# Attention over a graph's edges and the sums over edges behind it: another layout of the sums, one product on another engine, and another order of loads

## The chip, the cores and the metric

The kernel runs on one core of one Trainium2 chip. The metric is the device time of one execution in microseconds (us). Engines are named as the profile names them: PE is TensorE's matmul, PEld its weight load, DVE is VectorE, ACT is ScalarE, POOL is GpSimd and SP is SyncE, which here only issues transfers.

## The reference, cut to what matters

The program is a stack of eight layers over N = 3125 nodes with C = 256 features and E = 53125 edges. Three of them bear on the change. Layer 0 is attention over edges; layer 1's graph part and the two convolutions of layer 3's add, for every node, the rows of its neighbours times a weight of the edge:

```python
# layer 0: attention over edges (4 heads of 64)
e = attn_src[:, src_idx] + attn_dst[:, dst_idx]
e = jnp.where(e >= 0, e, NEG_SLOPE * e)
e = e * edge_weight[None, :]
e_exp = jnp.exp(e - jnp.max(e))
denom = jax.ops.segment_sum(e_exp.T, dst_idx, num_segments=num_nodes).T
alpha = e_exp / (denom[:, dst_idx] + 1e-10)
msg = h[:, src_idx] * alpha[..., None]
out = jax.vmap(lambda m: jax.ops.segment_sum(m, dst_idx, num_segments=num_nodes))(msg)
...
# layer 1, and twice in layer 3: a weighted sum over the edges
msg = x[src] * edge_weight[:, None]
agg = jax.ops.segment_sum(msg, dst, num_segments=x.shape[0])
```

## The kernel before

**Attention** (`attend_edges`). The edges lie sorted by their end in 25 rounds of 2125. In a round POOL gathers 17 tiles of rows by index (L1120), ACT makes masks from the ends of the edges, `dst_all` (L1181, L1183), PE adds the ends' terms (L1346), DVE makes the logits (L1262 to L1269), a maximum goes through PE and back (L1353, L1274), DVE scales the rows (L1283) and PE adds them up by node (L1371) with masks `spread` of DVE (L1255). Three sets of buffers go round. At the end DVE makes each node's share, `den` (L1324 to L1327), multiplies all the sums by it (L1329) and adds them to X (L1330).

SP's queue holds, beside the transfer of `dst_all` for each round (L1151), the loads of *blocks*. A block is the edges of five nodes, up to 125 of them; there are 625 blocks, and 630 loads of 120 rows (L1158) put them on chip, 30 for each of the rounds 0 to 20. What SP does is what its queue says, in order. When the loads are there, `block_keys` (L790) turns ends and starts into the numbers that the next stage compares. `begin_rest` and `pick_rest` (L750, L764) look for blocks with more than 120 edges.

**Counts and sums over edges** (`count_edges`). 125 batches of KB = 5 blocks. In a batch DVE makes one-hot rows of the starts, `low` (L885), and of the ends with the rest of the start, `cell` (L886), and the product of `low` with the edges' weights, `heavy` (L872, in `weighs`). PE multiplies `cell` by `low` into counts (L935) and `heavy` by `cell` into sums (L941); ACT copies both out of PSUM (L968, L973) to `total` and `sums`, the latter of 128 x 3125 numbers for a group of five batches. SP stores them in `edge_counts` and `edge_sums` (L995), a group at a time. The buffers between DVE and PE have five slots. Then a loop runs over the blocks with a rest: DVE marks the block as done and looks for the next (L911 to L773), the block's old counts and sums are loaded (L1014, L1015), added to (L919, L920) and stored again (L1017, L1018).

A block's sums have 125 columns: number d*25 + t stands for end d of the block (of 5) and part t of the starts (of 25).

**Aggregates** (`aggregate`, three times). It reads `edge_sums` back and multiplies: for each group and each half of the features 25 matmuls, one for each t, of a tile of features with the sums of that t (L728). Their moving operand has 250 columns (two groups x 25 blocks x 5 ends) of 4 bytes each:

```python
last = pe.matmul(acc[:, m, h, 0:groups * GD], M[:, t, h * 128:(h + 1) * 128], heavy[m][0:P, 0:groups, t],
                 start=(t == 0), stop=(t == T - 1))
```

Every such part of the program is a phase, and each phase ends with a barrier of all engines (L90). So the count loop starts when attention's last instruction is done.

Of the kernel before, what the change touches and what calls it, by code (L numbers as in the profile page):

```python
# [18 lines left out]
F32 = mybir.dt.float32  # L19
# [29 lines left out]
LOADED = 21  # L49
HELD = LOADS * LOADED  # L50
# [615 lines left out]
class SumsLoads(Ahead):  # L666


    def __init__(self, nc, stack, name, weights):
        super().__init__(nc, stack, name)  # L670
        self.first = self.sb("first", [128, 2, T, GD])
        self.weights = weights
# [6 lines left out]
def aggregate(nc, g, weights, M, AT, loads, turn=1, last=True, ahead=()):  # L679

    with Phase(nc) as ph:
        heavy = (loads.first, ph.sb("second", [ROWS, 2, T, GD]))
# [33 lines left out]
        def _(pe):  # L716
# [73 lines left out]
def block_keys(dve, then, own, based):  # L790


    src, dst = (own.edges[:, 0:BLOCKS, k] for k in (1, 0))
    then(dve.tensor_copy(own.spare, src))
# [5 lines left out]
    then(dve.tensor_copy(own.spare, dst))  # L800
# [7 lines left out]
def count_edges(nc, g, edges, own, counts, weights):  # L808
# [6 lines left out]
    with Phase(nc) as ph:  # L815
        low = ph.sb("low", [EB, SLOTS, KB, ROWS])
# [3 lines left out]
        sums = ph.sb("sums", [ROWS, 2, T, GD])  # L820
# [6 lines left out]
        old_counts = ph.sb("old_counts", [P, P], U16)  # L827
        added = ph.sb("added", [1, BLOCKS])
# [10 lines left out]
        sums_stored = [ph.sem(f"sums_stored{m}") for m in range(2)]  # L839
        rest_read = ph.sem("rest_read")  # L840
# [10 lines left out]
        old_sums = sums[0:P, 1]  # L851
# [17 lines left out]
        def weighs(eng, n, k):  # L869
            at = k % SLOTS  # L870
            eng.wait_ge(low_ready, n + 1)
            eng.tensor_tensor(heavy[:, at], low[:, at], own.edges[:, bass.ds(n * KB, KB), 2:3].bitcast(F32).to_broadcast([EB, KB, ROWS]),  # L872
                              ALU.mult).then_inc(heavy_ready, 1)


        @block.vector
        def _(dve):
            dve.sem_inc(batch_summed, SLOTS)
            dve.sem_inc(counts_kept, TURNS)
            dve.sem_inc(batch_kept, TURNS)  # L880
# [8 lines left out]
            over_batches(dve, one)  # L889

            rests = rest_total(dve)
            with dve.Fori(0, rests) as v:
                then = Steps(dve, rest_step, v * REST)
                b = dve.value_load(g.pick_i[0:1, 0:1], min_val=0, max_val=BLOCKS - 1)
                place = nc.s_assert_within(b % BG, 0, BG - 1, skip_runtime_bounds_check_because="a block's place in its group")
# [24 lines left out]
                then(dve.tensor_tensor(old_sums[:, :, bass.ds(place * BLK, BLK)], old_sums[:, :, bass.ds(place * BLK, BLK)],  # L920
                                       acc[0:P, 0, 1, 0, 0:P].rearrange("p (d h) -> p h d", h=T), ALU.add))
# [4 lines left out]
        def _(pe):  # L926
            def one(n, k, i):
# [29 lines left out]
        def _(act):  # L957
            def one(n, k, i):
# [21 lines left out]
        def _(sp):  # L980
# [22 lines left out]
            store(GROUPS - 1, 0)  # L1003
            for m in range(2):
                sp.wait_ge(sums_stored[m], 16 * (GROUPS // 2) + 32 - 16 * m)
                sp.wait_ge(stored[m], 32 * (GROUPS // 2) + 64 - 32 * m)
            with sp.Fori(0, rests) as v:
# [9 lines left out]
                sp.dma_start(old, old_sums.rearrange("p h d -> p (h d)")).then_inc(rest_stored, 16)  # L1017
# [12 lines left out]
SETS = 3  # L1030
# [3 lines left out]
def attend_edges(nc, g, table, a_dst, dst_flat, dst_row, edges, own_blocks, X):  # L1034
# [5 lines left out]
    with Phase(nc) as ph:  # L1040
# [20 lines left out]
        total = ph.sb("total", [P, T, W])  # L1061
        den = ph.sb("den", [P, T, HEADS])
# [80 lines left out]
        def _(sp):  # L1143
# [77 lines left out]
        def _(dve):  # L1221
# [1811 lines left out]
```

## Time and profile before

| | |
|---|---|
| median of 3 runs | 5204.59 us (5191.33, 5204.59, 5204.67) |
| profiled execution | 5195.46 us, span 5193.8 us |
| PE busy | 4168.2 us, 80% of the span |
| DVE busy | 2408.1 us, 46% |
| ACT busy | 1855.3 us, 36% |
| POOL busy | 862.5 us, 17% |
| mean granted TensorE clock | 0.883 of full speed |

The shares are means over many stages, each with a limit of its own. Attention runs from about 107 to 834.9 us of the span, the count loop to 1116.1 and its loop over rests to 1155.9 us, the first aggregate from 1524.4 to 1790.9 us, the two others from 4239 us on. Within a stage what counts is the engine that the others wait for.

### The profile page before, as it was taken

The page shows a single profiled execution, that of the slowest core. Times are in us where ns is not written, and L with a number is a line of the kernel's source. Part 1 is how long each engine was busy: PE and PEld are TensorE (multiplying, and loading weights), DVE is VectorE, ACT ScalarE, POOL GpSimd, SP SyncE. Part 2 cuts the span into 40 slices and gives each one's busy share as a digit, 9 for nine tenths or more (in the row PEclk, how much of TensorE's full clock was granted, in tenths as well). Part 3 has the DMA queues.
Part 4 walks back from the last instruction along what each step waited for, and adds up shares of the span by engine and source line. Part 5 has one row for each costly group of instructions (what it writes and reads, how often), then busy time and mean ns, then how long its engine had stood idle before and what let it go on. Part 6 is the DMA issues. An engine that isn't in the chain of part 4 may idle for free. (4 is left out here: it accounts for less than half of the span.)

```text
span 5193.8 us, 79246 instructions
## 1 busy us (share of the span) xinstructions
PE 4168.2 (80%) x22693; PEld 3605.1 (69%) x22694; DVE 2408.1 (46%) x4239; ACT 1855.3 (36%) x3178; POOL 862.5 (17%) x796
## 2 busy tenths in 40 slices
PE   2588877955749976967997998997499969899675
PEld 2476767954638843866886886886499858788554
DVE  5355558965340032126995995897411140110424
ACT  2333323642410032424664664665143310110322
POOL 2577770002600010210000000000122200000101
PEclk8688888986969988988998998998599979999788
DMA  3344432542343211321221221221312144133000
GB/s 102 84 114 116 121 90 98 214 172 64 107 140 148 86 33 38 125 72 41 57 54 33 58 57 32 54 56 24 91 60 80 51 132 159 75 150 148 13 18 27
DMA packets 459231, 440.36 MB, mean 85 GB/s; under 512 B 347128, under 2 KB 411341, under 8 KB 446050
## 3 DMA queue, kind: packets, MB, share of 16 engines
q1 hardware_dynamic: 423868, 341.36, 21.6%
q0 software_dynamic: 35232, 97.61, 6.5%
q8 instruction: 38, 0.62, 0.0%
q14 instruction: 93, 0.76, 0.0%
HBM read 342.44 MB, written 96.42 MB: 84 GB/s over the span
## 5 line engine op out<-in xcount | busy, mean ns | idle before, releaser
L2575 PE MATMUL p_acc<-p_H,p_eT 125*125 125x256 f32 x3750 | 823.6, 379 | 0.0
L2575 PEld LDWEIGHTS p_acc<-p_H,p_eT 125*125 125x125 f32 x3750 | 696.2, 187 | 105.0
L1120 POOL DMA_INDIRECT p_message<-edge_table,p_index x425 | 495.1, 1165 | 170.5 <-issue 119.5
L1371 PE MATMUL p_acc<-p_message,p_spread 125*125 125x260 f32 x1666 | 427.9, 424 | 33.9 <-issue 29.1
L2059 DVE BATCH_NORM_STATS2 features_stats<-F x60 | 29.2, 487 | 868.0 <-ACT F L2050 867.3
L1371 PEld LDWEIGHTS p_acc<-p_message,p_spread 125*125 125x125 f32 x1666 | 349.9, 212 | 104.1 <-issue 36.2
L1830 ACT ACTIVATE p_hid<-p_up,p_b1s 128x125 f32<-128x125 f32 x764 | 272.2, 365 | 398.4 <-PE p_up L1806 355.0
L1806 PEld LDWEIGHTS p_up<-p_xT,p_w1s 128*128 128x128 f32 x3056 | 377.6, 199 | 50.1 <-issue 33.8
L1806 PE MATMUL p_up<-p_xT,p_w1s 128*128 128x125 f32 x3056 | 385.0, 284 | 32.0 <-issue 14.0
L1814 PE MATMUL p_down<-p_w2s,p_hid 128*125 128x256 f32 x1528 | 361.3, 386 | 11.7 <-ACT p_hid L1830 10.5
L526 PE MATMUL p_turned<-identity,p_slot 125*128 125x125 f32 x400 | 89.1, 376 | 303.3 <-DVE p_slot L494 299.7
L1423 POOL IOTA p_order_i<- 125x200 int32 x3 | 1.1, 381 | 1974.9 <-SPq L88 1974.9
L2498 ACT ACTIVATE p_eT<-p_turned 125x500 f32<-125x500 f32 (+1 forms) x525 | 251.1, 539 | 203.2 <-PE p_turned L2568 186.5
L1814 PEld LDWEIGHTS p_down<-p_w2s,p_hid 128*125 128x125 f32 x1528 | 278.0, 190 | 58.1 <-ACT p_hid L1830 17.6
L740 ACT ACTIVATE AT<-p_acc 128x250 f32 (+1 forms) x78 | 28.9, 371 | 772.6 <-PE p_acc L728 772.6
L526 PEld LDWEIGHTS p_turned<-identity,p_slot 125*128 125x128 f32 x400 | 59.8, 188 | 333.1 <-DVE p_slot L494 330.0
L728 PE MATMUL p_acc<-sums_first,H 125*128 125x250 f32 (+1 forms) x1400 | 278.0, 359 | 5.4 <-PEq L721 5.4
L728 PEld LDWEIGHTS p_acc<-sums_first,H 125*128 125x128 f32 x1400 | 248.0, 189 | 34.0 <-PEq L718 6.2
L2428 DVE CUSTOM_DVE_ANT_0 p_e_room<-p_S,p_pen 125x3125 f32<-125x3125 f32 x75 | 256.2, 3416 | 19.2 <-DVE p_pen L2422 15.6
L2438 DVE SCALAR_TENSOR_TENSOR p_e_room<-p_e_room,p_H,p_e_low 125x3125 f32<-125x3125 f32 x75 | 260.0, 3467 | 10.2 <-ACT p_e_low L2484 9.0
L2447 DVE CUSTOM_DVE_ANT_0 p_e_room<-p_e_room,p_count 125x3125 f32<-125x3125 f32 x75 | 256.2, 3416 | 12.4 <-ACT p_e_room L2490 8.9
L2490 ACT ACTIVATE p_e_room<-p_e_room,p_minus 125x3125 f32<-125x3125 f32 x75 | 217.7, 2903 | 116.3 <-DVE p_e_room L2438 116.3
(492 smaller groups left out, 6794.8 us busy)
## 6 DMA issues: line engine op xcount, KB each, us to landing
sums_first<-edge_sums SPq DMA_DIRECT2D x39, 1562.5 KB
p_count<-edge_counts SPq DMA_DIRECT2D x375, 152.6 KB
p_second<-edge_sums SPq DMA_DIRECT2D x36, 1562.5 KB, 8.0
edge_sums<-p_sums SPq DMA_DIRECT2D x25, 1562.5 KB
edge_counts<-p_total SPq DMA_DIRECT2D x25, 683.6 KB
p_w1s<-in_L_ffn_W SPq DMA_DIRECT2D x16, 1024.0 KB
p_got<-made SPq DMA_DIRECT2D x25, 560.0 KB
p_dst_all<-dst_row SPq DMA_DIRECT2D x25, 531.2 KB
```

Of the source, the lines that this page charges most:

```text
L728: last = pe.matmul(acc[:, m, h, 0:groups * GD], M[:, t, h * 128:(h + 1) * 128], heavy[m][0:P, 0:groups, t], start=(t == 0), stop=(t == T - 1))
L1120: pool.indirect_dma_start(message[:, m, k, :], None, table, bass.IndirectOffsetOnAxis(ap=index[:, m, k:k + 1], axis=0)).then_inc(landed[m] ...
L1371: last = pe.matmul(at, spread[:, k], message[0:P, m, k], start=(k == 0), stop=(k == R_CH - 1))
L1806: last = pe.matmul(up[:, c % 4, 0:UN], w1s[:, s, h, c * 128:(c + 1) * 128], xT[:, h], start=(h == 0), stop=(h == KH - 1))
L1814: last = pe.matmul(down[:, 0:C], hid[:, c], w2s[:, s, c], start=(c == 0), stop=(c == HC - 1))
L1830: act.activation(hid[:, c], up[:, c % 4, 0:UN], ACT.Gelu, bias=b1s[:, s, c:c + 1]).then_inc(hid_ready, 1)
L2428: dve.tensor_tensor_reduce(out=e[:, s], in0=S[:], in1=pen[:], scale=1.0, scalar=0.0, op0=ALU.add, op1=ALU.max, accum_out=peak[:, s:s + 1]) ...
L2438: dve.scalar_tensor_tensor(out=e[:, k % 2], in0=e[:, k % 2], scalar=d_of(t), in1=e_low[:], op0=ALU.add, op1=ALU.max).then_inc(leaky_ready, 1)
L2447: dve.tensor_tensor_reduce(out=e[:, s], in0=e[:, s], in1=count[:, k % 3], scale=1.0, scalar=0.0, op0=ALU.mult, op1=ALU.add, accum_out=den[ ...
L2490: act.activation(e[:, s], e[:, s], ACT.Exp, bias=minus[:, s:s + 1]).then_inc(raised, 1)
L2498: act.activation(eT[:, r % 4, 0:n], turned[:, r % 4, 0:n * P].rearrange("p (a n) -> p a n", a=n), ACT.Copy).then_inc(run_kept, 1)
L2575: last = pe.matmul(acc[:, s, 0:C], eT[:, r % 4, a % 4], H[:, a, 0:C], start=(a == 0), stop=(a == T - 1))
```

## The change

What it does, in six parts:

1. `sums`, and with it `edge_sums`, keeps each block's 125 columns as they come out of PSUM, in place of putting together the columns of one t over all blocks. ACT's copy (L973) becomes contiguous. The aggregates' moving operand then takes every 25th number, 100 bytes apart.
2. `weighs` goes from DVE to POOL. `low` has 125 columns in place of 128, and the three last columns of `heavy` are cleared once.
3. The product of the sums with the share and the sum with X leave the end of attention. DVE does them a tile at a time in the count loop, two instructions of 125x256 after every fifth batch.
4. In SP's queue the load of `dst_all` for round r stands ahead of the loads of blocks of round r - 3, for every round; before, the loads of blocks of rounds 0, 1 and 2 stood ahead of `dst_all` of round 3. There are 660 loads of blocks in place of 630.
5. On DVE `begin_rest` stands behind round 18, `pick_rest` behind 19, the first half of `block_keys` (`block_lows`) behind 21 and the second behind 22, in place of all of the first two behind 22 and of `block_keys` behind 23.
6. The last group is stored batch by batch, and the loop over rests loads and stores 125x125 of the sums in place of 125x3125.

```diff
 def aggregate(nc, g, weights, M, AT, loads, turn=1, last=True, ahead=()):
...
-                        last = pe.matmul(acc[:, m, h, 0:groups * GD], M[:, t, h * 128:(h + 1) * 128], heavy[m][0:P, 0:groups, t],
+                        last = pe.matmul(acc[:, m, h, 0:groups * GD], M[:, t, h * 128:(h + 1) * 128], heavy[m][0:P, 0:groups, :, t],
...
 def count_edges(...):
-            eng.tensor_tensor(heavy[:, at], low[:, at], own.edges[:, bass.ds(n * KB, KB), 2:3].bitcast(F32).to_broadcast([EB, KB, ROWS]),
+            eng.tensor_tensor(heavy[:, at, :, 0:P], low[:, at], own.edges[:, bass.ds(n * KB, KB), 2:3].bitcast(F32).to_broadcast([EB, KB, P]),
                               ALU.mult).then_inc(heavy_ready, 1)
+
+        @block.gpsimd
+        def _(pool):
+            over_batches(pool, lambda n, k, i: weighs(pool, n, k))
...
+            dve.memset(heavy[:].rearrange("p s b l -> p (s b) l")[:, :, P:ROWS], 0.0).then_inc(cleared, 1)
...
-                dve.tensor_tensor(low[:, at], lanes(ROWS), each(own.low, n, ROWS), ALU.is_equal).then_inc(low_ready, 1)
+                dve.tensor_tensor(low[:, at], lanes(P), each(own.low, n, P), ALU.is_equal).then_inc(low_ready, 1)
                 dve.tensor_tensor(cell[:, at], lanes(P), each(own.key, n, P), ALU.is_equal).then_inc(cell_ready, 1)
-                weighs(dve, n, k)
...
+                if k % IN_GROUP == IN_GROUP - 1:
+                    t = i * (PER // IN_GROUP) + k // IN_GROUP
+                    o = attended[0][:, tile(t), 0:C].rearrange("p a (h o) -> p (a h) o", h=HEADS)
+                    dve.tensor_tensor(o, o, attended[1][:, tile(t), :].rearrange("p a h -> p (a h)").unsqueeze(2).to_broadcast([P, HEADS, HO]), ALU.mult).then_inc(shared, 1)
+                    dve.wait_ge(shared, t + 1)
+                    x = X[:, tile(t), :].rearrange("p a c -> p (a c)")
+                    dve.tensor_tensor(x, x, attended[0][:, tile(t), 0:C].rearrange("p a c -> p (a c)"), ALU.add)
...
-                    a = (s * KB + first) * BLK
-                    last = act.activation(sums[:, m, :, a:a + many * BLK],
-                                          acc[:, k % TURNS, 1, bank, 0:many * P].rearrange("p (b d h) -> p h (b d)", b=many, h=T), ACT.Copy)
+                    a = s * KB + first
+                    last = act.activation(sums[:, m, a:a + many].rearrange("p b l -> p (b l)"), acc[:, k % TURNS, 1, bank, 0:many * P], ACT.Copy)
...
-            store(GROUPS - 1, 0)
+            for s in range(IN_GROUP):
+                done, part = BATCHES - IN_GROUP + TURNS + s + 1, slice(s * KB * P, (s + 1) * KB * P)
+                sp.wait_ge(counts_kept, done)
+                split_rows(sp, counts[N - P:N, part], total[:, 0].rearrange("p b l -> p (b l)")[:, part], stored[0])
+                sp.wait_ge(batch_kept, done)
+                sp.dma_start(weights[(GROUPS - 1) * ROWS:GROUPS * ROWS, part], sums[:, 0].rearrange("p b l -> p (b l)")[:, part]).then_inc(sums_stored[0], 16)
...
-                old = weights[bass.ds(group * ROWS, P), :]
-                sp.dma_start(old_sums.rearrange("p h d -> p (h d)"), old).then_inc(old_loaded, 16)
+                old = weights[bass.ds(group * ROWS, P), bass.ds(place * P, P)]
+                sp.dma_start(old_sums[:], old).then_inc(old_loaded, 16)
...
 def attend_edges(...):
-            for r in range(SETS):
-                blocks_of(r)
-            with sp.Fori(1, LOADED // SETS) as i:
+            with sp.Fori(1, ROUNDS // SETS) as i:
                 for m in range(SETS):
                     one(i * SETS + m, i, m)
-                    blocks_of(i * SETS + m)
-            for r in range(LOADED, ROUNDS):
+                    blocks_of((i - 1) * SETS + m)
+            for r in range(ROUNDS // SETS * SETS, ROUNDS):
                 one(r, r // SETS, r % SETS)
+                blocks_of(r - SETS)
...
+                if coming == 6:
+                    begin_rest(dve, rest_then, g, own_blocks.low[0:1], own_blocks.spare_i[0:1], own_blocks.spare[0:1, 0:1])
+                if coming == 5:
+                    pick_rest(dve, rest_then, g, own_blocks.low[0:1])
+                if coming == 3 and isinstance(r, int):
+                    dve.wait_ge(own_edges_loaded, 16 * HELD)
+                    block_lows(dve, rest_then, own_blocks)
                 if coming == 2:
-                    over = own_blocks.low[0:1]
-                    begin_rest(dve, then, g, over, own_blocks.spare_i[0:1], own_blocks.spare[0:1, 0:1])
-                    pick_rest(dve, then, g, over)
-                if coming == 1:
-                    dve.wait_ge(own_edges_loaded, 16 * HELD)
-                    block_keys(dve, then, own_blocks, based)
+                    block_keys(dve, rest_then, own_blocks, based)
...
-            o = total[:, :, 0:C].rearrange("p t (h o) -> p t h o", h=HEADS)
-            then(dve.tensor_tensor(o, o, den[:].unsqueeze(3).to_broadcast([P, T, HEADS, HO]), ALU.mult))
-            then(dve.tensor_tensor(X[:], X[:], total[:, :, 0:C], ALU.add))
```

The first place is DVE at the end of attention (`p_den` is the share, `p_total` the sums) and the head of the count loop. Before:

```order
L1329 TENSOR_TENSOR p_total<-p_total,p_den 125x25x256
L1330 TENSOR_TENSOR X<-X,p_total 125x6400
L88 UNCONDITIONAL_BRANCH
L876 UNCONDITIONAL_BRANCH
L854 UNCONDITIONAL_BRANCH
L854 ISA
L885 ISA
L885 TENSOR_TENSOR p_low<-XT 128x640
L886 ISA
L886 TENSOR_TENSOR p_cell<-XT 128x625
L872 ISA
L872 TENSOR_TENSOR p_heavy<-p_low,XT 128x640
```

And in the changed kernel, where `attended` is the sums, `attended_share` the share, and L878 the product that DVE no longer has:

```order
L1351 TENSOR_TENSOR attended_share<-attended_share,p_peak_of 125x100
L88 UNCONDITIONAL_BRANCH
L886 UNCONDITIONAL_BRANCH
L889 MEMSET p_heavy 128x25x3
L860 UNCONDITIONAL_BRANCH
L860 ISA
L896 ISA
L896 TENSOR_TENSOR p_low<-XT 128x625
L897 ISA
L897 TENSOR_TENSOR p_cell<-XT 128x625
```

DVE's end of attention is two instructions of 6400 elements shorter, and a batch has two instructions in place of three. The tile's pair stands behind every fifth batch:

```order
L896 ISA
L896 TENSOR_TENSOR p_low<-XT 128x625
L897 ISA
L897 TENSOR_TENSOR p_cell<-XT 128x625
L904 ISA
L904 REGISTER_ALU
L904 TENSOR_TENSOR attended<-attended,attended_share 125x256
L905 REGISTER_ALU
L907 ISA
L907 TENSOR_TENSOR X<-X,attended 125x256
L895 REGISTER_ALU
```

The second place is POOL in the count loop, which stood empty there before; it now makes one product in every batch:

```order
L860 UNCONDITIONAL_BRANCH
L860 ISA
L878 ISA
L878 TENSOR_TENSOR p_heavy<-p_low,XT 128x5x125
L877 REGISTER_ALU
L878 ISA
```

The third place is SP's queue at attention's start. Before, three transfers of the ends (`p_dst_all`) are followed by the loads of blocks into `XT`:

```order
L1144 DMA p_own<-in_dst_flat 125x425
L1146 DMA dst_row<-p_own 125x425
L1151 DMA p_dst_all<-dst_row 128x2125 x3
L189 TENSOR_LOAD block_starts
L1158 ISA
L1158 DMA XT<-in_edges 120x4
L1158 ISA
L1158 DMA XT<-in_edges 120x4
```

After it, a fourth transfer of the ends stands ahead of the first load of a block:

```order
L1166 DMA p_own<-in_dst_flat 125x425
L1168 DMA dst_row<-p_own 125x425
L1173 DMA p_dst_all<-dst_row 128x2125 x3
L1186 UNCONDITIONAL_BRANCH
L1186 ISA
L1173 ISA
L1173 DMA p_dst_all<-dst_row 128x2125
L189 ISA
L189 TENSOR_LOAD block_starts
L1180 ISA
L1180 DMA XT<-in_edges 120x4
```

## Rows read from the trace of the kernel before

**Rows 1.** Windows, by stage: stretch, its us, then each engine's busy us (instructions)

```profile
834.90:1116.10 281.20, 278.67 (x2500) 278.51 (x2500) 276.14 (x387) 190.79 (x500) 0.00 (x0) 0.99 0.53 203
1116.10:1155.90 39.80, 0.69 (x4) 0.51 (x4) 6.19 (x14) 0.25 (x1) 0.00 (x0) 0.52 0.36 140
1524.40:1790.90 266.50, 266.29 (x1300) 237.91 (x1300) 0.00 (x0) 9.53 (x26) 0.00 (x0) 0.99 0.36 140
```

**Rows 2.** Timeline, attention's start: start, us, instruction, [idle before, releaser]

```profile
127.41 63.39 SPq L1158 DMA_DIRECT2D XT<-in_edges  x90
191.13 0.37 SPq L1151 DMA_DIRECT2D p_dst_all<-dst_row  x1
...
195.06 2.07 ACT L1181 ACTIVATE p_far<-p_dst_all,p_node 125x2125 bf16<-125x2125 int16 x1 [36.53 <-DMA p_dst_all<-dst_row]
...
199.68 2.43 PE L1346 MATMUL p_term<-p_a_part,p_from_dst 125*125 x17 [31.30 <-ACT p_from_dst L1183]
...
180.30 0.22 DVE L1269 TENSOR_REDUCE p_part_max<-p_logit 125x1 f32<-125x68 f32 x1
212.19 0.28 DVE L1274 TENSOR_REDUCE p_top<-p_small 1x1 f32<-1x125 f32 x1 [31.67 <-PE p_small L1353]
```

**Rows 3.** Timeline, attention's end, DVE and one row of PE

```profile
723.00 0.23 DVE L1266 TENSOR_TENSOR p_logit<-p_logit,p_message 125x68 f32<-125x68 f32 x1 [2.67 <-DMA p_message<-edge_table,p_index]
...
749.41 0.23 DVE L1266 TENSOR_TENSOR p_logit<-p_logit,p_message 125x68 f32<-125x68 f32 x1 [2.80 <-DMA p_message<-edge_table,p_index]
...
780.08 0.23 DVE L1266 TENSOR_TENSOR p_logit<-p_logit,p_message 125x68 f32<-125x68 f32 x1
...
805.33 10.44 PE L1371 MATMUL p_acc<-p_message,p_spread 125*125 125x260 f32 x34 [4.80 <-DVE p_spread L1255]
...
819.41 6.83 DVE L1329 TENSOR_TENSOR p_total<-p_total,p_den 125x6400 f32<-125x6400 f32 x1
826.27 6.83 DVE L1330 TENSOR_TENSOR X<-X,p_total 125x6400 f32<-125x6400 f32 x1
```

**Rows 4.** Timeline, two batches of the count loop

```profile
899.88 0.82 DVE L872 TENSOR_TENSOR p_heavy<-p_low,XT 128x640 f32<-128x640 f32 x1
...
900.61 0.82 DVE L885 TENSOR_TENSOR p_low<-XT 128x640 f32<-128x640 f32 x1
...
902.07 0.83 DVE L872 TENSOR_TENSOR p_heavy<-p_low,XT 128x640 f32<-128x640 f32 x1
```

**Rows 5.** Timeline, behind the count loop, SP and DVE

```profile
1116.14 0.36 SPq L995 DMA_DIRECT2D edge_sums<-p_sums  x1
...
1125.14 0.54 DVE L911 TENSOR_SCALAR p_added<-block_number,picked_block 1x625 f32<-1x625 f32 x1 [11.79 <-SPq L986]
...
1130.92 0.14 DVE L773 CAST picked_block_i<-picked_block 1x1 int32<-1x1 f32 x1
1139.46 0.29 DVE L919 TENSOR_TENSOR p_old_counts<-p_old_counts,p_acc 125x125 uint16<-125x125 uint16 x1 [8.40 <-DMA p_old_counts<-edge_counts]
```

**Rows 6.** Timeline, POOL's products of two operands and a DVE instruction beside one

```profile
4890.48 2.54 POOL L2165 TENSOR_TENSOR p_slot<-p_slot,XT 128x625 f32<-128x625 f32 x2 [0.65 <-ACT p_slot L2156]
...
5147.50 13.66 POOL L2807 TENSOR_TENSOR X<-X,p_gain 125x6400 f32<-125x6400 f32 x1 [215.34 <-DMA p_gain<-in_L_ffn_beta]
...
5151.55 9.68 DVE L404 TENSOR_TENSOR p_mean<-p_stats 125x25 f32<-125x25 f32 x1
```

**Rows 7.** Groups with their shapes, conversions of block_keys (L800 and L794 read every fourth number)

```profile
L800 DVE CAST XT<-XT 128x625 f32<-128x625 int32 x1 | 0.8, 751 | 0.0
L794 DVE CAST XT<-XT 128x625 f32<-128x625 int32 x1 | 0.7, 727 | 0.3 <-DVE p_total L1299 0.3
L803 DVE CAST XT<-XT 128x625 f32<-128x625 int32 x1 | 0.5, 486 | 0.0
```

**Rows 8.** The same view, layer norm (L406 reads both operands every sixth number)

```profile
L406 DVE TENSOR_TENSOR p_diff<-p_stats 125x25 f32<-125x25 f32 x1 | 0.2, 204 | 0.0
L407 DVE TENSOR_TENSOR p_diff<-p_diff 125x25 f32<-125x25 f32 x1 | 0.2, 188 | 0.0
```

More of the change, by code:

```diff
@@ L48 @@
 LOADS = 30
-LOADED = 21
-HELD = LOADS * LOADED
+SETS = 3
+HELD = LOADS * ((CH // (CH // T)) - SETS)
 STARTS = 6 * P
@@ L670, in __init__ @@
         super().__init__(nc, stack, name)
-        self.first = self.sb("first", [128, 2, T, GD])
+        self.first = self.sb("first", [128, 2, GD, T])
         self.weights = weights
@@ L681, in aggregate @@
     with Phase(nc) as ph:
-        heavy = (loads.first, ph.sb("second", [ROWS, 2, T, GD]))
+        heavy = (loads.first, ph.sb("second", [ROWS, 2, GD, T]))
         acc = ph.psum("acc", [128, 2, KH, 512])
@@ L787, in __init__, with block_lows @@
         self.spare_i = at[4].bitcast(I32)
-def block_keys(dve, then, own, based):
-    src, dst = (own.edges[:, 0:BLOCKS, k] for k in (1, 0))
-    then(dve.tensor_copy(own.spare, src))
+def block_lows(dve, then, own):
+    then(dve.tensor_copy(own.spare, own.edges[:, 0:BLOCKS, 1]))
     then(dve.tensor_scalar(own.base, own.spare, 4195.0, None, ALU.mult))
@@ L799, in block_keys @@
     then(dve.scalar_tensor_tensor(out=own.low, in0=own.base, scalar=-float(P), in1=own.spare, op0=ALU.mult, op1=ALU.add))
-    then(dve.tensor_copy(own.spare, dst))
+def block_keys(dve, then, own, based):
+    then(dve.tensor_copy(own.spare, own.edges[:, 0:BLOCKS, 0]))
     then(dve.scalar_tensor_tensor(out=own.spare, in0=own.spare, scalar=float(T), in1=own.base, op0=ALU.mult, op1=ALU.add))
@@ L805, in block_keys, with count_edges @@
     then(dve.tensor_copy(own.lane, own.lane_i))
-def count_edges(nc, g, edges, own, counts, weights):
+def count_edges(nc, g, edges, own, attended, X, counts, weights):
     SLOTS = 5
@@ L815, in count_edges @@
     with Phase(nc) as ph:
-        low = ph.sb("low", [EB, SLOTS, KB, ROWS])
+        low = ph.sb("low", [EB, SLOTS, KB, P])
         cell = ph.sb("cell", [EB, SLOTS, KB, P])
@@ L819, in count_edges @@
         total = ph.sb("total", [P, 2, BG, P], U16)
-        sums = ph.sb("sums", [ROWS, 2, T, GD])
+        sums = ph.sb("sums", [ROWS, 2, BG, P])
         rest = ph.sb("rest", [EB, 4], I32)
@@ L919, in _ @@
                 then(dve.tensor_tensor(old_counts[:], old_counts[:], acc[0:P, 0, 0, 0, 0:P], ALU.add))
-                then(dve.tensor_tensor(old_sums[:, :, bass.ds(place * BLK, BLK)], old_sums[:, :, bass.ds(place * BLK, BLK)],
-                                       acc[0:P, 0, 1, 0, 0:P].rearrange("p (d h) -> p h d", h=T), ALU.add))
+                then(dve.tensor_tensor(old_sums[:], old_sums[:], acc[0:P, 0, 1, 0, 0:P], ALU.add))
                 dve.sem_inc(rest_added, 1)
@@ L926, in _ @@
         def _(pe):
+            pe.wait_ge(cleared, 1)
             def one(n, k, i):
@@ L934, in one @@
                     for q in range(many):
-                        last = pe.matmul(at_bank[0:P, 0, bank, q * P:(q + 1) * P], cell[:, at, first + q], low[:, at, first + q, 0:P], start=True, stop=True)
+                        last = pe.matmul(at_bank[0:P, 0, bank, q * P:(q + 1) * P], cell[:, at, first + q], low[:, at, first + q], start=True, stop=True)
                 last.then_inc(batch_counted, 1)
@@ L994, in store @@
                 sp.wait_ge(batch_kept, j * IN_GROUP + (IN_GROUP + TURNS))
-                sp.dma_start(weights[bass.ds(j * ROWS, ROWS), :], sums[:, m].rearrange("p h d -> p (h d)")).then_inc(sums_stored[m], 16)
+                sp.dma_start(weights[bass.ds(j * ROWS, ROWS), :], sums[:, m].rearrange("p b l -> p (b l)")).then_inc(sums_stored[m], 16)
                 split_rows(sp, counts[bass.ds(j * P, P), :], total[:, m].rearrange("p b l -> p (b l)"), stored[m])
@@ L1105, in over_groups, with over_pipeline @@
                     one(i * SETS + m, i, m)
-        def over_pipeline(eng, one):
-            with eng.Fori(0, ROUNDS // SETS - 1) as i:
+        def over_pipeline(eng, one, single=1):
+            with eng.Fori(0, ROUNDS // SETS - single) as i:
                 for m in range(SETS):
                     one(i * SETS + m, i, m, SETS)
-            for r in range((ROUNDS // SETS - 1) * SETS, ROUNDS):
+            for r in range((ROUNDS // SETS - single) * SETS, ROUNDS):
                 one(r, r // SETS, r % SETS, ROUNDS - 1 - r)
```

31 lines of the change are left out of this document (17 added, 14 removed).

## The prediction

> **What bounds the kernel now.** The page comes first: PE is busy for 80% of the span, but that is a mean over stages, and the change touches four of them. So I read the windows by stage, then in each the timeline, to see who waits for whom. In the count loop PE is busy for 278.67 of 281.20 us and DVE for 276.14 [rows 1]: both are full, and PE sets the pace with 281.20 / 125 = 2.25 us a batch. In the aggregate PE is busy for 266.29 of 266.50 us, at the full clock [rows 1]: whatever is added to a matmul there is added to the time. Behind the count loop stand 39.80 us in which PE works for 0.69 [rows 1]; SP's transfers and DVE's small steps follow each other. Attention is paced in its middle by POOL's gathers, and the change doesn't touch these; it touches its start, where ACT waited 36.53 us for one transfer [rows 2], and its end, where DVE alone works at the last 13.7 us [rows 3].
>
> The sum is made against the profiled execution's own 5195.5 us. Of the three runs shown two are 9 us above it and one is 4 below, so I add 6 at the end.
>
> **a) The load of the ends ahead of the blocks: -31 us.** SP issues 90 loads of blocks in 63.39 us, and only then, at 191.13, the ends of round 3; ACT starts on them at 195.06, PE at 199.68, DVE has its maximum at 212.19 [rows 2]. DVE was done with the logits of the round before at 180.52 and needed only PE's transpose, which stood in PE's queue behind the terms of round 3: the wait is 31.67 us [rows 2]. With the transfer issued some 60 us earlier, ahead of the loads, PE's terms are ready when DVE comes. The wait goes whole but for the usual 0.5 us. What is late next is POOL's gather, which comes every 25 to 26 us (DVE's waits on landings end at 723.00 and 749.41, 26.4 apart [rows 3]); it waited for the buffers that this stall held, and moves up by the same. The 30 loads that each later round issues are no more than the 30 that it issued before, 0.70 us each (63.39 / 90 [rows 2]), 21 of 26 us. Bounds: -31, and -20 if part of the stall comes back at POOL.
>
> **b) The end of attention: -23 us.** DVE's logits of the last round start at 780.08 with no wait, 26.4 us behind 749.41 they would have at 775.8 [rows 3]; begin_rest and pick_rest stood between. Ahead of them goes -4. `block_keys` made PE wait 4.80 us at 805.33 [rows 3]: -5. L1329 and L1330 are 6.83 us each, with all other engines done [rows 3]: -13.7. What is inserted at rounds 18 to 22 is some 4 us a round; DVE's waits on landings there are 2.80 us and the like [rows 3], and they hide most of it. The wait for all 660 loads of blocks, added at round 21, has behind it on DVE the rest of that round and so everyone; the loads are issued by then, since a round's 30 take 21 us of its 26. Bounds: -23 and -18.
>
> **c) The last store and the rest: -14 us.** From the store at 1116.14 to DVE's start at 1125.14 are 9.0 us [rows 5]; of that store a fifth is left at the end, -6. DVE is ready with its search at 1131.06 and waits 8.40 us for the old sums, 1.5 MB, until 1139.46 [rows 5]; of 125x125 numbers it is a twenty-fifth, and it is there first: -8. Bounds: -8 and -20.
>
> **d) The product on POOL: +63 us.** DVE starts an instruction every 0.73 us and a batch every 2.19 (899.88, 900.61, 902.07 [rows 4]); it loses one of three, and gains the tile's two of 256 columns, by the slope below 0.42 us each, for five batches: 2 x 0.73 + 0.17 = 1.63 us a batch, well under 2.25. POOL's product of 128x625 takes 2.54 / 2 = 1.27 us [rows 6], also well under. If they ran side by side PE would keep the pace and this edit were free. But one row says they don't: a DVE product of 125x25 beside POOL's 13.66 us product began at 5151.55 and ended at 5161.23, after 9.68 us, within 0.1 us of POOL's end at 5161.16 [rows 6], where the same kind of instruction takes 204 ns otherwise [rows 8]. Both read two operands from SBUF, as here. Then the two take turns: 1.63 + 1.27 = 2.90 us a batch; the fixed part of an instruction, 0.15 us (below), can overlap, and I take 2.75. 125 x (2.75 - 2.25) = +63. Behind POOL's product waits PE's sums, behind these ACT and the slots, five deep; PE's new wait for the memset of 75 columns costs some 0.2 us once. Bounds: 0 (side by side) and +110 (3.1 us, if each change of turns costs something more; PE would also be idle for a quarter of the time, and the clock, 0.99 now [rows 1], might fall).
>
> The Trainium skill, page "SBUF — State Buffer", section "Who interferes with whom", says that a DVE instruction with two SBUF inputs and a GpSimd instruction that reads SBUF exclude each other, for the whole instruction. By that rule, the trace agrees, at 9.68 us in place of 0.2, and the edit would cost the 2.90 us in full, +81.
>
> **e) The strided read: +45 us.** No matmul of the kernel before reads its moving operand with gaps, so the price is bounded by what other engines show. The aggregate spends 266.29 us [rows 1] on 1200 instructions of 250 columns and 100 of 125, 312,500 columns: 0.852 ns each. Three aggregates have 937,500. DVE's slope first: 6.83 us for 6400 elements [rows 3] and 0.82 for 640 [rows 4] give 1.04 ns an element and 0.15 us fixed. DVE's conversions of 625 take 486 ns contiguous and 751 and 727 with gaps [rows 7]. Less the fixed part, a read with gaps takes 0.92 to 0.96 ns. Of the products in rows 8, 204 against 188 ns for 25 elements with two reads each, it is 1.04 + 0.64 = 1.68 for two, 0.84 for one. If a read with gaps takes its 0.84 to 0.96 ns whoever reads, PE, which asks for one in 0.852, hardly feels it: 0 to +101 us. I take 0.90 ns, +45. If the gap's cost came on top of PE's own time, 0.42 ns (751 - 486 over 625), it would be +394.
>
> ACT's contiguous copy, `low`'s three columns less and the one memset change nothing that others wait for: ACT is busy for 190.79 of 281.20 us [rows 1].
>
> **Sum.** 5195.5 - 31 - 23 - 14 + 63 + 45 = 5235.5, with 6 for the median 5242 us. 0.3%, about what a measurement here can tell from no change, is 16 us.
>
> **Rivals.**
> *Stride doubles the matmul (slower by far).* The ratio, not the absolute time, carries over: DVE's conversion went from (486 - 150) / 625 = 0.54 to 0.94 ns, a factor of 1.75, and a factor of 2 on PE is 0.852 x 937,500 = +799. For it: a matmul stream has no slack in the aggregate, PE 266.29 of 266.50 [rows 1]. Against it: PE's instruction reads 4 bytes only every 0.852 ns, more slowly than DVE's conversion did. Time: 5990 to 6045.
> The Trainium skill, page "SBUF — State Buffer", section "Specifications (TRN2)", gives lines of 16 bytes, of which two hits are needed for full bandwidth; here no line is hit twice, and by that rule this rival is what happens. The trace agrees for DVE (751 against 486 ns) and says nothing of PE.
> *The gap's cost comes on top*: +300 to +394, 5500 to 5590.
> *Stride free*, the rest as forecast: 5197, no change.
> *POOL runs beside DVE (faster).* The place is the count loop: if the exclusion hits only long or differently placed operands, the batch stays at 2.25 us and d) is 0. With e) at +45 the time is 5179, with e) at 0 it is 5134. It decides below a batch of 2.35 us. Against it stands the one clear row of rows 6.
>
> **Chances.** Forecast (turns taken, 0.84 to 0.96 ns a column) 0.35, its own range 5210 to 5310; doubled 0.33; on top 0.06; stride free 0.14; POOL beside DVE 0.12. To hold 8 in 10 the range must reach from the stride-free case into the doubled one: 5175 to 6045. Faster is the last case, 0.12. Same is the stride-free one and the low edge of the forecast, 0.16. Slower is the rest, 0.72.
>
> **What would show it.** a) PE's and DVE's waits near 180 to 212 us gone, the count loop's start some 54 us earlier. b) No instruction of 6.8 us at attention's end. c) 39.80 us of tail at some 25. d) The count loop's window: 344 us for turns taken, with PE busy for 80% and POOL for more than 1.27 us a product; 281 us if side by side. e) The aggregate's window: 266 us if free, 281 as forecast, 530 if doubled. The forecast is wrong above all if e) is: it is the one price with no row of its own engine.

## The result and the profile after

The changed kernel takes 6062.05 us (median of 4 runs, 6061.07 to 6070.27) against 5201.89 us: a ratio of 1.1671, 95% interval 1.1657 to 1.1685, 860 us slower. The profiled execution's span is 6061.0 us. From its page, busy time by engine:

```profile
PE 5078.1 (84%) x22693; PEld 3708.7 (61%) x22694; DVE 2449.9 (40%) x4163; ACT 1855.1 (31%) x3178; POOL 1072.2 (18%) x921
```

PE's busy time has grown by 910 us, more than the whole loss; what else changed is small beside it. The same windows as in [rows 1], and the two later aggregates (stretch, its us, then busy us of PE, PEld, DVE, ACT, POOL with their instructions, then the clock, the DMA engines' share and GB/s):

```profile
782.10:1117.20 335.10, 306.25 (x2500) 287.21 (x2500) 329.87 (x300) 187.81 (x498) 203.01 (x125) 0.99 0.46 174
1117.20:1135.00 17.80, 0.94 (x7) 0.56 (x5) 8.41 (x25) 0.75 (x2) 0.00 (x0) 0.64 0.24 75
1503.60:2066.00 562.40, 560.97 (x1302) 271.79 (x1303) 0.00 (x0) 9.68 (x26) 0.00 (x0) 1.00 0.17 66
4514.00:5074.50 560.50, 560.47 (x1300) 271.21 (x1300) 0.00 (x0) 9.40 (x25) 0.00 (x0) 1.00 0.17 66
5147.60:5708.10 560.50, 560.45 (x1300) 271.15 (x1300) 0.00 (x0) 9.41 (x26) 0.00 (x0) 1.00 0.17 66
```

The first aggregate takes 560.3 us in place of 266.50 (its window of 562.40 reaches 2 us into the next part of the program, hence x1302), at the same clock, and PE is busy all through it. The two later ones take 560.5 us each; before, the first of them stood so:

```profile
4239.30:4504.00 264.70, 264.63 (x1300) 236.68 (x1300) 0.00 (x0) 9.40 (x26) 0.00 (x0) 1.00 0.36 140
```

and the second the same, 264.7. Together that is 294 + 2 x 296 = 886 us. The count loop has grown from 281.20 to 335.1 us, with PE idle for 29 us of it, and the 39.80 us behind it are 17.8. The loop itself starts at 782.1 in place of 834.90, 53 us earlier. The sum, -53 + 54 - 22 + 886 = +865, is the change of the span, 867 us, within 2.

Attention's start, SP's queue and DVE at the maximum, which answer to [rows 2]:

```profile
126.48 0.35 SPq L1173 DMA_DIRECT2D p_dst_all<-dst_row  x1
128.78 20.61 SPq L1180 DMA_DIRECT2D XT<-in_edges  x30
...
181.01 0.22 DVE L1290 TENSOR_REDUCE p_part_max<-p_logit 125x1 f32<-125x68 f32 x1
...
181.70 0.28 DVE L1295 TENSOR_REDUCE p_top<-p_small 1x1 f32<-1x125 f32 x1 [0.46 <-PE p_small L1374]
```

The ends of round 3 are asked for at 126.48, ahead of the loads, and DVE's wait for the maximum is 0.46 us in place of 31.67.

The count loop, one batch with a tile's pair and one without, which answers to [rows 4]:

```profile
859.70 0.80 DVE L897 TENSOR_TENSOR p_cell<-XT 128x625 f32<-128x625 f32 x1
...
859.97 1.62 POOL L878 TENSOR_TENSOR p_heavy<-p_low,XT 128x625 f32<-128x625 f32 x1 [0.86 <-DVE p_low L896]
860.42 1.45 DVE L904 TENSOR_TENSOR attended<-attended,attended_share  x1
...
862.01 0.42 DVE L907 TENSOR_TENSOR X<-X,attended  x1
862.53 0.81 DVE L896 TENSOR_TENSOR p_low<-XT 128x625 f32<-128x625 f32 x1
...
863.25 0.80 DVE L897 TENSOR_TENSOR p_cell<-XT 128x625 f32<-128x625 f32 x1
863.54 1.61 POOL L878 TENSOR_TENSOR p_heavy<-p_low,XT 128x625 f32<-128x625 f32 x1 [1.95 <-DVE p_low L896]
863.98 1.84 DVE L896 TENSOR_TENSOR p_low<-XT 128x625 f32<-128x625 f32 x1
```

While POOL makes its product DVE's instruction is held: L896 takes 1.84 us in place of 0.81, and L904 1.45 in place of 0.42. POOL, for its part, starts 0.53 us before `cell` (L897) ends and needs 1.6 us for a product that holds DVE for 1.03. So a batch is 0.72 + 0.72 + 1.03 = 2.47 us, and the tile's pair makes it 2.68 on the mean (335.1 / 125).

The end of the count loop, which answers to [rows 5]:

```profile
1119.03 0.63 SPq L1027 DMA_DIRECT2D edge_sums<-p_sums  x1
1123.44 0.33 SPq L1038 DMA_DIRECT2D p_old_sums<-edge_sums  x1
1124.05 0.29 SPq L1039 DMA_DIRECT2D p_old_counts<-edge_counts  x1
...
1130.17 0.29 SPq L1042 DMA_DIRECT2D edge_counts<-p_old_counts  x1
...
1123.04 0.53 DVE L930 TENSOR_SCALAR p_added<-block_number,picked_block 1x625 f32<-1x625 f32 x1 [1.87 <-SPq L1005]
...
1129.08 0.29 DVE L938 TENSOR_TENSOR p_old_counts<-p_old_counts,p_acc 125x125 uint16<-125x125 uint16 x1
...
1135.24 1.08 DVE L398 BATCH_NORM_STATS2 p_stats<-X  x3 [5.56 <-PEq L90]
```

The old sums come in the time that DVE needs for its search anyway: L938 has no wait in place of 8.40 us. DVE's next part of the program (L398) starts 6.2 us behind L938; before, its first instruction stood 16.4 us behind the same sum, which began at 1139.46 [rows 5]:

```profile
1155.86 0.43 DVE L398 BATCH_NORM_STATS2 p_stats<-X  x1 [15.57 <-PEq L90]
```

The matmul of the aggregate, grouped by shape, with its busy time:

```profile
L728 PE MATMUL p_acc<-sums_first,XN 125*128 125x250 f32 x600 | 269.8, 627 | 3.3 <-PEq L721 3.3
```

269.8 us of busy time for 600 instructions of 250 columns is 450 ns each, 1.80 ns a column; before it was 0.852. (The 627 ns are the mean length of one record; the instructions overlap, so the pace is read from the busy time.)

### The profile page after: what moved, and what is told of

Same layout as the page of the kernel before. It is cut to its first block and busy times, and to the rows that moved or that the text cites. A ratio compares the mean times of both kernels' runs of the same rounds, so it can differ in the third digit from the quotient of the medians.

```text
span 6061.0 us, 79618 instructions
## 1 busy us (share of the span) xinstructions
PE 5078.1 (84%) x22693; PEld 3708.7 (61%) x22694; DVE 2449.9 (40%) x4163; ACT 1855.1 (31%) x3178; POOL 1072.2 (18%) x921
## 5 line engine op out<-in xcount | busy, mean ns | idle before, releaser
L728 PE MATMUL p_acc<-sums_first,H 125*128 125x250 f32 (+1 forms) x1400 | 585.8, 596 | 5.4 <-PEq L721 5.4
L728 PE MATMUL p_acc<-p_second,H 125*128 125x250 f32 x1200 | 539.5, 627 | 0.0
L728 PEld LDWEIGHTS p_acc<-sums_first,H 125*128 125x128 f32 x1400 | 292.8, 209 | 296.2 <-issue 284.0
L1392 PE MATMUL p_acc<-p_message,p_spread 125*125 125x260 f32 x1666 | 424.5, 422 | 28.8 <-issue 28.8
L728 PEld LDWEIGHTS p_acc<-p_second,H 125*128 125x128 f32 x1200 | 249.6, 208 | 287.8 <-issue 287.8
L2186 POOL TENSOR_TENSOR p_slot<-p_slot,XT 128x625 f32<-128x625 f32 x20 | 27.9, 1420 | 2016.9 <-ACT p_slot L2177 2016.9
L728 PE MATMUL p_acc<-sums_first,XN 125*128 125x250 f32 (+1 forms) x700 | 292.9, 596 | 3.3 <-PEq L721 3.3
L728 PE MATMUL p_acc<-p_second,XN 125*128 125x250 f32 x600 | 269.6, 627 | 0.0
```

The source lines that it names most:

```text
L1392: last = pe.matmul(at, spread[:, k], message[0:P, m, k], start=(k == 0), stop=(k == R_CH - 1))
L2186: pool.tensor_tensor(o, o, XT[:, h, i * GN:(i + 1) * GN], ALU.add).then_inc(joined, 1)
```

## The experiments

Two questions were open: what a read with gaps costs PE, and by what rule; and whether DVE and POOL take turns because of what they read. The other kernels take the change apart. A ratio to before is to the kernel before as it was measured along with that run: 5195.11 us for the layout undone, the layout alone, the product back on DVE and SP's order alone, 5191.46 us for the last two kernels. The kernels that change only the step or POOL's instruction ran once each, and are read by their windows alone. Some of the code below is shortened.

### The layout undone

```diff
-heavy[m][0:P, 0:groups, :, t]
+heavy[m][0:P, 0:groups, t]
-last = act.activation(sums[:, m, a:a + many].rearrange("p b l -> p (b l)"), acc[:, k % TURNS, 1, bank, 0:many * P], ACT.Copy)
+last = act.activation(sums[:, m, :, a:a + many * BLK], acc[:, k % TURNS, 1, bank, 0:many * P].rearrange("p (b d h) -> p h (b d)", b=many, h=T), ACT.Copy)
```

Expected: 

> The changed kernel with the old layout of the sums (ACT takes them apart, the aggregates read contiguous columns), and so with the old last store and the old loads of the rest. Theory 1, the strided read alone costs 2 x per column: the three aggregates go back from 562 us each to 266, minus 888, the tail from 17.8 us back to some 40, plus 22: 6062 - 888 + 22 = 5196 us. Rival, the layout also helped the count loop through ACT's cheaper copy: the count loop then grows beyond 335 us, and the time lies above 5205.

Measured 5199.86 us, ratio to before 1.0012 (1.0002 to 1.0022). Its windows of the count loop and the first aggregate:

```profile
782.40:1118.00 335.60, 306.50 (x2500) 287.28 (x2500) 329.91 (x300) 190.14 (x499) 202.91 (x125) 0.99 0.44 171
1525.70:1792.00 266.30, 266.27 (x1300) 237.73 (x1300) 0.00 (x0) 9.38 (x25) 0.00 (x0) 0.99 0.36 140
```

The aggregate is back at 266.3 us, and the count loop stays at 335.6. So the layout carries the whole loss of the aggregates and nothing of the count loop's; ACT's cheaper copy was worth nothing there. The old last store and the old loads of the rest came back with the old layout.

### The layout alone

The kernel before with only these lines turned the other way, and the sum of the rest written to fit.

Expected: 

> The kernel before with the new layout alone (ACT's copy contiguous, the aggregates' moving operand at every 25th number; the rest's loads stay whole). Theory 1: plus 888 us in the three aggregates and nothing else, 5202 + 888 = 6090 us. Rival, ACT's cheaper copy (0.12 us less a batch at most) shows in the count loop: up to 15 us less than that.

Measured 6082.92 us, ratio 1.1709 (1.1686 to 1.1733). Its first aggregate:

```profile
1524.70:2085.00 560.30, 560.28 (x1300) 271.33 (x1300) 0.00 (x0) 9.37 (x25) 0.00 (x0) 1.00 0.17 67
```

+888 us against the 5195.11 of before, as expected, now without any other part of the change.

### Steps of 2, 3, 4 and of 5, 8, 16 numbers

```diff
-heavy[m][0:P, 0:groups, t]
+flat[m][:, t:t + step * (n - 1) + 1:step]    # n = groups * GD columns, another step in each aggregate
```

Expected of the first: 

> The kernel before, with the same number of columns in each aggregate, but read with a step: every 2nd number (8 bytes) in the first aggregate, every 3rd (12 bytes) in the second, every 4th (16 bytes) in the third. The sums over edges are then of wrong columns; the amount of work is the same. Contiguous columns take 0.852 ns each and every 25th takes 1.80. Theory 1, two numbers out of one 16-byte line are needed: 0.85 at step 2, something between at step 3, 1.8 at step 4; the aggregates take 266, 300 to 450, and 560 us. Rival A, any gap costs in full: 1.8 at all three. Rival B, the cost grows with the distance: 1.0 or less at all three, and only wide steps reach 1.8.

Its three aggregates, each in a window of its own:

```profile
1526.00:1805.60 279.60, 279.55 (x1300) 238.58 (x1300) 0.00 (x0) 9.37 (x25) 0.00 (x0) 0.99 0.35 134
4256.60:4672.50 415.90, 415.85 (x1300) 254.91 (x1300) 0.00 (x0) 9.39 (x26) 0.00 (x0) 1.00 0.23 89
4747.40:5299.90 552.50, 552.50 (x1300) 270.92 (x1300) 0.00 (x0) 9.37 (x25) 0.00 (x0) 1.00 0.17 67
```

Expected of the second: 

> The same at steps 5, 8 and 16 (20, 32 and 64 bytes). The sums are again of wrong columns. Theory 1: 1.8 ns a column at all three, 562 us an aggregate. Rival B, the cost grows with the distance: under 1.8 at 5 and 8, and rising. Rival C, steps of a power of two are worse than 25: more than 1.8 at 8 and 16.

```profile
1525.20:2085.40 560.20, 560.13 (x1300) 271.96 (x1300) 0.00 (x0) 9.41 (x26) 0.00 (x0) 1.00 0.17 67
4538.80:5102.10 563.30, 563.30 (x1300) 271.76 (x1300) 0.00 (x0) 9.38 (x25) 0.00 (x0) 1.00 0.17 66
5177.00:5704.20 527.20, 527.07 (x1300) 268.90 (x1300) 0.00 (x0) 9.46 (x26) 0.00 (x0) 1.00 0.18 70
```

Over 312,500 columns: 0.895 ns a column at 8 bytes, 1.331 at 12, 1.768 at 16, 1.79 at 20, 1.80 at 32, 1.69 at 64, and 1.79 at 100 bytes in the changed kernel. From 8 to 16 bytes the times stand as 2.02 : 3.01 : 4, as do the pieces of 16 bytes that a column begins at these steps (a half, three quarters, one); above 16 bytes nothing more is added. So these steps fit a price of some 1.77 ns for each new piece of 16 bytes (1.69 at 64 bytes), and below 0.48 pieces a column (0.852 / 1.77, an estimate) that would hide behind the matmul's own pace; the next experiment shows how far this rule goes. Any gap in full and a cost that grows with the distance (rivals A and B) are out, and steps of a power of two are no worse. The Trainium skill, page "SBUF — State Buffer", section "Specifications (TRN2)", has this as lines of 16 bytes that want at least two hits each for full bandwidth; for PE's moving operand the trace nearly agrees, 0.895 ns with two hits, 5% above contiguous columns, and 1.77 with one.

### The other operand, pairs and fives

```diff
-M[:, t, h * 128:(h + 1) * 128], heavy[m][0:P, 0:groups, t]
+M.flat[:, at:at + 25 * 127 + 1:25], heavy[m][0:P, 0:groups, t]    # first aggregate
+M[:, t, h * 128:(h + 1) * 128], pairs of neighbours, a pair in 50   # second
+M[:, t, h * 128:(h + 1) * 128], five neighbours, five in 125        # third
```

Expected: 

> The kernel before with other patterns, all on wrong columns: in the first aggregate the weights (the stationary operand, 128 columns) are read at every 25th number and the moving operand contiguous; in the second the moving operand is read in pairs of neighbours, one pair in 50 numbers; in the third in runs of five neighbours, one in 125 numbers. Theory 1, two hits on a line are enough, and only the moving operand's stream sets the time: first aggregate, a weight load at 1.8 instead of 0.85 ns a column takes 128 x 0.95 = 0.12 us more, which is hidden beside a matmul of 0.21 us, so 266 us; second 266 us (all columns in pairs); third at most 1.2 ns a column, 375 us. Rival: the loads aren't hidden, the first aggregate takes 266 + 1300 x 0.12 = 425 us; or pairs cost as much as singles, 562 us in the second.

```profile
1529.80:1842.10 312.30, 312.30 (x1300) 311.29 (x1300) 0.00 (x0) 9.37 (x25) 0.00 (x0) 0.99 0.31 120
4301.90:4596.80 294.90, 294.87 (x1300) 240.33 (x1300) 0.00 (x0) 9.37 (x25) 0.00 (x0) 0.99 0.33 126
4669.70:4953.70 284.00, 283.95 (x1300) 237.81 (x1300) 0.00 (x0) 9.37 (x25) 0.00 (x0) 1.00 0.34 131
```

And the first aggregate's matmuls by shape, two of three groups:

```profile
L754 PE MATMUL p_acc<-sums_first,XN 125*128 125x250 f32 x600 | 146.3, 405 | 3.3 <-PEq L747 3.3
L754 PE MATMUL p_acc<-sums_first,XN 125*128 125x125 f32 x100 | 23.9, 401 | 0.0
```

Weights at every 25th number: 312.3 us, and now PEld is busy all through, 311.29 of it. A matmul of 125 columns now comes every 239 ns (23.9 / 100) and one of 250 every 244 (146.3 / 600), so the load sets the pace: one of 128 columns costs 240 ns (312.3 / 1300), 1.87 a column. That is close to the 1.8 I had put in, but I compared only the 0.12 us more with the matmul's 0.21. The whole load has to fit beside it, and 27 ns of it stick out behind each of the 1200 matmuls of 213 ns, and more behind the 100 short ones. The rival's 425 us is out, and so is "hidden".

Pairs: 294.9 us, 0.94 ns a column, where the aggregate took 264.7 us before. (The 100 matmuls of 125 columns stayed contiguous.) It is not the 562 of singles, but 11% above contiguous columns and 5% above the step of 8 bytes, though both begin half a piece a column; this stays open. Fives: 284.0, well below 375, but 7% above 264.7. A run of 20 bytes touches two pieces, 0.4 a column, and by the rule above that should hide whole. If each piece cost the larger of 1.77 ns and 0.85 ns for each number taken out of it, with nothing evened out between neighbours, it would be some 0.95 ns a column, 296 us, an estimate from these times. The 284 lie between the two readings, and no run decides.

### POOL without its reads

```diff
-eng.tensor_tensor(heavy[:, at, :, 0:P], low[:, at], weights of the edges, ALU.mult)
+eng.memset(heavy[:, at, :, 0:P], 1.0)                                  # first kernel
+eng.tensor_scalar(heavy[:, at, :, 0:P], low[:, at], 0.5, None, ALU.mult)   # second kernel
```

Expected of the fill: 

> The changed kernel, but POOL fills the product's buffer with a constant (it writes 128 x 625 numbers and reads none) in place of multiplying; the sums over edges are wrong. Theory 1, what POOL and DVE take turns at is reading two operands from SBUF against POOL's reading: with no read on POOL's side DVE's first comparison takes 0.81 us again in place of 1.84, and the count loop is PE's at 281 to 285 us. Rival, they exclude each other in whatever they do in SBUF: DVE's 1.84 us stays about as it is, less only what a fill is shorter than a product.

The count loop's window and three instructions of it:

```profile
783.60:1065.00 281.40, 278.48 (x2502) 278.32 (x2503) 210.82 (x312) 188.49 (x500) 78.04 (x125) 0.99 0.54 207
```

```profile
860.52 0.81 DVE L896 TENSOR_TENSOR p_low<-XT 128x625 f32<-128x625 f32 x1 [0.68 <-PE p_acc L961]
...
861.24 0.80 DVE L897 TENSOR_TENSOR p_cell<-XT 128x625 f32<-128x625 f32 x1
...
861.45 0.62 POOL L879 MEMSET p_heavy<- 128x625 f32 x1 [1.58 <-DVE p_low L896]
```

The fill begins at 861.45, in the middle of L897, and takes 0.62 us; L897 takes 0.80. So neither waits for the other, though both are at work for 0.59 us, and the loop is PE's, 281.4 us. So it is POOL's reading that holds DVE.

Expected of the product with a constant: 

> The changed kernel, but POOL multiplies by a constant and so reads one operand in place of two; the sums over edges are wrong. Theory 1, any POOL instruction that reads SBUF excludes DVE's two-operand comparison: DVE's first comparison still takes more than 0.81 us, by the time that POOL's instruction holds on. Rival, only two reads against two reads collide: it takes 0.81 us and the count loop is at 281 us, as with the fill.

Groups with count, busy time and mean:

```profile
L879 POOL TENSOR_SCALAR p_heavy<-p_low 128x625 f32<-128x625 f32 x122 | 247.2, 2050 | 17.8 <-DVE p_low L896 17.7
L896 DVE TENSOR_TENSOR p_low<-XT 128x625 f32<-128x625 f32 x120 | 128.9, 1074 | 17.1 <-PE p_acc L961 15.2
L897 DVE TENSOR_TENSOR p_cell<-XT 128x625 f32<-128x625 f32 x121 | 96.8, 800 | 0.0
```

The mean of L896, 1.07 us, mixes two lengths, as its timeline shows, with the loop's window above it:

```profile
783.60:1065.00 281.40, 278.17 (x2503) 277.80 (x2502) 250.90 (x310) 188.50 (x500) 251.88 (x125) 0.99 0.55 210
...
788.54 1.31 DVE L896 TENSOR_TENSOR p_low<-XT 128x625 f32<-128x625 f32 x1
789.77 0.80 DVE L897 TENSOR_TENSOR p_cell<-XT 128x625 f32<-128x625 f32 x1
790.49 0.92 DVE L904 TENSOR_TENSOR attended<-attended,attended_share  x1
...
791.90 0.80 DVE L896 TENSOR_TENSOR p_low<-XT 128x625 f32<-128x625 f32 x1
```

Where POOL holds DVE, L896 takes 1.30 us in place of 0.81 and L904 0.92 in place of 0.42, 0.50 more each time; elsewhere it takes its 0.80. So one operand read by POOL is enough to hold DVE, as theory 1 has it, but for 0.50 us of an instruction that is itself some 2.0 long. Why so little of it is open. The rival's time came true all the same: 0.72 + 0.72 + 0.50 is 1.94 us a batch, below PE's 2.25, and the loop is at 281.4 us.

### The product back on DVE

Expected: 

> The kernel with the old layout, and the product with the weights back on DVE as well; the attention's last two products stay in the count loop. Theory 1, DVE and POOL take turns in the count loop and that is all that made it longer: a batch goes from 2.67 to 3 x 0.72 + 0.17 + waits = 2.35 us, now DVE's own, minus 40: 5196 - 40 = 5156 us. Rival, the count loop's pace came from the semaphores between three engines and not from the shared access: then POOL's part gone gives the full way back to 2.25 us a batch or less, minus 53, 5143 us.

```diff
-        @block.gpsimd
-        def _(pool):
-            over_batches(pool, lambda n, k, i: weighs(pool, n, k))
...
                 dve.tensor_tensor(cell[:, at], lanes(P), each(own.key, n, P), ALU.is_equal).then_inc(cell_ready, 1)
+                weighs(dve, n, k)
```

Measured 5161.75 us, ratio to before 0.9938 (0.9921 to 0.9954), 38 us less than with POOL.

```profile
780.70:1080.30 299.60, 283.48 (x2500) 279.73 (x2500) 290.70 (x430) 190.89 (x500) 0.00 (x0) 0.99 0.50 191
```

299.6 us, 2.40 a batch, with DVE busy for 290.70: DVE's own pace, as the theory had it, and 18 us above PE's. So attention's 13.7 us are not saved in the count loop: DVE was full there.

### SP's order alone

The kernel before with part 4 of the change only, and still 630 loads of blocks.

Expected: 

> The kernel before with the new order of SP's queue alone: the ends of a round ahead of the blocks' loads. Theory 1: the 31.7 us stall at 180 to 212 us is gone and none of it comes back, 5202 - 31 = 5171 us. Rival, POOL's later rounds or the loads of blocks, which now end later, take a part back: 5180 us or more.

Measured 5160.05 us, ratio 0.9935 (0.9918 to 0.9951).

```profile
800.80:1082.10 281.30, 278.68 (x2500) 278.52 (x2500) 276.13 (x387) 190.91 (x500) 0.00 (x0) 0.99 0.53 203
```

The count loop starts at 800.8 in place of 834.90, 34 us earlier: the stall is gone and nothing of it comes back.

### The share on ACT, and the rest's block alone

```diff
+            def share(t, h):
+                o = attended[0][:, tile(t), h * HO:(h + 1) * HO].rearrange("p a o -> p (a o)")
+                act.activation(o, o, ACT.Copy, scale=attended[1][:, tile(t), h:h + 1].rearrange("p a h -> p (a h)")).then_inc(shared, 1)
...
+                if not isinstance(n, int) and s < HEADS:
+                    share(i * (PER // IN_GROUP) + j + 1, s)
```

Expected of the first: 

> As the version with the old layout and the product on DVE (5162 us), but the product of attention's sums with the share is made by ACT in the count loop, a head of a tile in each batch, one tile ahead, and DVE keeps only the sum with X. Theory: the count loop there was DVE's, 3 x 0.72 + 0.17 + waits = 2.37 us a batch; with 0.08 in place of 0.17 it is back at PE's 2.25, minus 8 to 14 us: 5150 us. Rival: ACT's copies are what PE waits for with only two turns in PSUM, and 0.25 us more of ACT in a batch cost PE as much: 5162 or more.

Measured 5136.6 us, ratio 0.9887 (0.9870 to 0.9905). Its count loop and what stands behind:

```profile
782.30:1063.30 281.00, 278.41 (x2500) 278.22 (x2500) 280.42 (x412) 212.55 (x599) 0.00 (x0) 0.99 0.53 204
1063.30:1103.30 40.00, 0.69 (x4) 0.51 (x4) 6.26 (x14) 0.17 (x1) 0.00 (x0) 0.56 0.36 139
```

281.0 us: PE has the loop again, with the tile's work inside it at no cost, and ACT's 212.55 us leave room. It gained 18.6 us in the loop, more than the 8 to 14 of the theory, since the whole of DVE's excess went; the medians are 25 apart, the profiled spans 15.6.

```diff
-old = weights[bass.ds(group * ROWS, P), :]
+old = weights[bass.ds(group * ROWS, P), :].rearrange("p (h d) -> p h d", h=T)[:, :, bass.ds(place * BLK, BLK)]
```

Expected of the second: 

> The same, and the loop over rests loads and stores only the block's numbers out of the old layout, 125 x 25 runs of 20 bytes, in place of 1.5 MB. Theory: DVE's wait of 8.6 us for the old sums shrinks and the store behind it too, minus 8 us: 5142 us. Rival: 3125 pieces of 20 bytes take as long as 1.5 MB in long rows: no change or slower.

Measured 5126.06 us, ratio 0.9868 (0.9850 to 0.9886), the fastest of all: 1.3% below the kernel before.

```profile
1063.50:1092.30 28.80, 0.69 (x4) 0.51 (x4) 6.26 (x14) 0.18 (x1) 0.00 (x0) 0.58 0.44 89
```

28.8 us behind the loop in place of 40.00, and DVE waits 1.28 us for the old sums in place of 8.66. 3125 runs of 20 bytes come sooner than 1.5 MB in long rows, so the small load did not need the new layout.

## Why the prediction was wrong

**a) The ends ahead of the blocks.** Right. -31 predicted; the wait of 31.67 us is gone, and alone it gave 34 us on the count loop's start.

**b) The end of attention.** The loop starts 53 us earlier, a) and b) together, where -54 stood. With the 34 of a) alone, 19 are left for b), where -23 stood: that the sum fits within 1 is in part luck, since the two misses cancel. The 13.7 us of the two long instructions are right for that place only.

**c) The last store and the rest.** -14 predicted, -22 measured, just beyond the bound of -20. The wait of 8.40 us went as predicted. The last store gave less than its -6: DVE's search starts 5.8 us behind the loop (1123.04 against 1117.2) in place of 9.0, -3. What I had put at nothing is the store back of the old sums, a twenty-fifth as well: from the sum to the next part of the program it was 16.4 us and is 6.2, -10; with the layout undone, and with it the whole transfers back, it is 16.4 again (1142.28 to 1158.72).

**d) The product on POOL.** Mechanism right, +63 predicted, +54 measured (335.1 - 281.20). The term that was a little off is POOL's share of the turn: 1.27 us less an overlap of 0.15, 1.12, where POOL holds DVE for 1.03. That the holding comes of POOL's reads is shown by the fill.

**e) The strided read.** This failed. The step was: "If a read with gaps takes its 0.84 to 0.96 ns whoever reads, PE, which asks for one in 0.852, hardly feels it: 0 to +101 us. I take 0.90 ns, +45." It carried an absolute time from DVE to PE. The runs show that PE has a time of its own for a column that lies in a new piece of 16 bytes, 1.69 to 1.80 ns at steps of 16 bytes and more, some 2.1 times its pace on contiguous columns: 1.79 ns a column here, +886 us. The rival that carried the ratio over, with 0.33, gave 5990 to 6045. It was short by what 2.1 is more than 2, +886 in place of +799, 87 us; that c) and d) came out 17 us cheaper than forecast hid a part of it. The additive rival (+0.42 ns) is out: +0.94 was added. The trace of before had no matmul with gaps, as I said; I gave the larger chance to the reading under which PE's slower pace protects it. The steps of 8, 12 and 16 bytes show that this pace protects only up to about half a piece a column, and the pairs and fives that it does so only nearly.

The range ended at 6045, 17 us short. It followed from a factor of exactly 2 at its upper edge.

## What to carry to other kernels

When a layout is made contiguous for one reader, count the other readers' columns: here ACT's copy saved nothing, since ACT waited, and PE, which bound three stages alone, paid 0.94 ns for each of 937,500 columns. In these runs a matmul's moving operand with gaps cost 5 to 11% as long as it took at least two numbers of 4 bytes out of each 16, and 2.1 times with one; the step of 12 bytes, one or two numbers out of each, cost 57%. A product given to an idle POOL isn't free where DVE reads two operands: compare what POOL holds (1.03 us) with what DVE sheds (0.72), and look first at the engine that has room of another kind, here ACT.

## What the runs showed of the hardware that was not expected

- PE's time for a column in a new 16-byte piece of the moving operand is 1.77 ns, against DVE's 0.92 to 0.96 ns a number with gaps [rows 7]; DVE's figure did not carry over to PE.
- The step of 64 bytes is a little cheaper (1.69 ns) than 16, 20, 32 or 100 (1.77 to 1.80). Why was not tried.
- Weights read with gaps cost the same a column (1.87 ns), but 128 of them, 240 ns, are mostly covered by a matmul of 250 columns, 213 ns: 312.3 us in place of 266.
- A POOL instruction that writes 128x625 numbers and reads none does not hold DVE's comparisons at all; one that reads one operand holds them for 0.50 us where they meet (0.26 on the mean), one that reads two for 1.03.
